# A bias spread and a padding copy moved, and identity products placed in the gaps of a decoder kernel's filling and emptying steps

## The reference

```python
x = x + L0_attn(layernorm(x))                  # self attention, window of +-32 tokens, biases
x = x + L0_xattn(ctx, ctx, layernorm(x), pad)  # cross attention, a padding mask an item, biases
x = x + L0_ffn(layernorm(x))                   # 8 experts, best 2 of a token
x = x + L1_attn(layernorm(x))                  # self attention, causal, no biases
x = x + L1_xattn(layernorm(x), ctx, ctx, mask) # cross attention, one mask, biases
x = x + L1_ffn(layernorm(x))                   # gate, up and down, quantised and dequantised
```

## Time and profile before

| what | value |
|---|---|
| median of 3 runs | 2112.07 us (2107.06 to 2112.2) |
| the profiled execution | 2101.48 us |
| its span, first to last instruction | 2099.7 us |
| its mean granted TensorE clock | 0.975 |
| TensorE busy, share of the span | 93% |
| VectorE, ScalarE, GpSimd busy | 59%, 47%, 33% |

### The profile page before, as it was taken

One profiled execution on the slowest core, in us unless ns is written; L12 is line 12 of the kernel. 1 busy time (PEld: TensorE's weight loads), 2 busy tenths in 40 slices (PEclk: granted clock), 3 DMA queues, 4 the chain that ended last, 5 costly groups with the idle time before them and its releaser, 6 DMA issues. The chain is left out here.

```text
span 2099.7 us, 57083 instructions
## 1 busy us (share of the span) xinstructions
PE 1948.5 (93%) x19802; PEld 1597.3 (76%) x19802; DVE 1233.8 (59%) x5200; ACT 979.4 (47%) x1905; POOL 686.7 (33%) x1244
## 2 busy tenths in 40 slices
PE   7999998999959999999999789999899998999889
PEld 5788886777749999999999578887677775444377
DVE  5788885676541111111115588998778886369964
ACT  2555555676613333333333255556566663357400
POOL 2666665256560000000001545553422220013400
PEclk8999999999969999999999999999999999999999
DMA  7333332334339999999995534433233330000023
GB/s 217 110 109 112 120 129 83 103 113 135 104 120 402 376 339 344 344 340 341 339 343 221 176 119 146 130 125 128 88 96 114 110 108 27 0 0 0 0 71 91
DMA packets 209555, 334.74 MB, mean 159 GB/s; under 512 B 59502, under 2 KB 193427, under 8 KB 200307
## 3 DMA queue, kind: packets, MB, share of 16 engines
q1 hardware_dynamic: 194914, 301.82, 41.6%
q0 software_dynamic: 9552, 26.10, 4.1%
q10 hardware_dynamic: 4928, 4.72, 0.7%
HBM read 193.74 MB, written 28.05 MB: 106 GB/s over the span
## 5 line engine op out<-in xcount | busy, mean ns | idle before, releaser
L2369 ACT ACTIVATE moe_h<-moe_h_ps,moe_weights 128x128 f32<-128x128 f32 x424 | 132.8, 364 | 255.5 <-PE moe_h_ps L2337 226.0
L2802 PE MATMUL ffn_prod_ps<-x_sb,ffn_weights 128*128 128x512 f32 x480 | 209.4, 596 | 7.0 <-ACT ffn_sig_q L2788 7.0
L2401 DVE TENSOR_TENSOR moe_y<-moe_y_ps,moe_weights 128x256 f32<-128x256 f32 x53 | 22.5, 425 | 328.1 <-PE moe_y_ps L2349 328.1
L2280 POOL DMA_DIRECT2D moe_y_dram<-moe_y x71 | 39.4, 555 | 491.4 <-DVE moe_y L2401 483.2
L1403 ACT ACTIVATE causal_prob<-causal_ps 128x768 f32<-128x768 f32 (+1 forms) x192 | 168.8, 879 | 63.0 <-PE causal_ps L1726 62.2
L2337 PE MATMUL moe_h_ps<-moe_h,moe_weights 128*128 128x128 f32 x1696 | 198.0, 275 | 0.0
L2337 PEld LDWEIGHTS moe_h_ps<-moe_h,moe_weights 128*128 128x128 f32 x1696 | 193.6, 192 | 0.1
L2802 PEld LDWEIGHTS ffn_prod_ps<-x_sb,ffn_weights 128*128 128x128 f32 x480 | 90.6, 191 | 123.6 <-issue 109.3
L1072 DVE CUSTOM_DVE_ANT_0 causal_masked<-causal_ps,causal_causal_mask 128x256 bf16<-128x256 f32 (+1 forms) x512 | 151.9, 353 | 28.6 <-PE causal_ps L1692 27.7
L1072 DVE CUSTOM_DVE_ANT_0 window_masked<-window_ps,window_window_mask 128x160 bf16<-128x160 f32 x512 | 135.1, 320 | 46.3 <-PE window_ps L1692 44.9
L1692 PE MATMUL causal_ps<-k_pair,q_pair 64*128 64x78 f32 (+2 forms) x1024 | 102.2, 299 | 20.5 <-DVE causal_m_tok L1072 9.3
(11 more groups left out here) (424 smaller groups left out, 4753.4 us busy)
## 6 DMA issues: line engine op xcount, KB each, us to landing
moe_weights<-moe_w_in SPq DMA_DIRECT2D x53, 2180.0 KB, 9.8
q_pair<-parts SPq DMA_DIRECT2D x512, 128.0 KB
parts<-moe_w_in SPq DMA_DIRECT2D x17, 2180.0 KB, 9.1
k_pair<-parts SPq DMA_DIRECT2D x256, 128.0 KB
k_pair<-parts SPq DMA_DIRECT2D x256, 38.5 KB
moe_y_dram<-moe_y POOLq DMA_DIRECT2D x71, 128.0 KB, 4.0
moe_rows<-moe_slots_dram SPq DMA_DIRECT2D x53, 128.0 KB, 3.7
x_before_ffn_dram<-x_sb SPq DMA_DIRECT2D x16, 256.0 KB, 2.1
```

The source lines that it names most:

```text
L2280: pool.dma_start(route.y_dram[bass.ds(j * TM, TM), :].rearrange("(s p) d -> p s d", p=P), y[r][:])\
L2369: nc.scalar.activation(out[:, f, :], psum[:, f // 2, (f % 2) * TM:(f % 2) * TM + TM], ACT.Gelu, bias=bias[:, f:f + 1]).then_inc(done, 1)
L2802: op = nc.tensor.matmul(prod_ps[:, slot, f, :].rearrange("p (b t) -> p b t", b=2), w[:, k, at:at + P], x_cols(n // GROUPS, k), start=(k == ...
```

## The change

Four edits. (1) `widen` keeps only the spread of bv and runs a slot earlier; the copy of the finished bias is a new function `keep_bias` in the old slot. (2) `padding` stands in slot 3 in all steps. (3) In step 1 of each call, ahead of slots 1 and 2, TensorE makes 5 identity products behind a wait for the values of item 0, and in step 18, ahead of slot 0, 5 more behind a wait for the turned outputs of item 14. (4) The 4 and 2 identity products around `turn_outputs` depend on `ref >= N + 2` alone, and so are made in step 34 of the first call too; the second call has them as before. The words that go with the change speak of fewer products in emptying steps; the code takes none away.

```diff
-        START_WARM, END_WARM, LOAD_WARM, DRAIN_WARM = 16, 13, 6, 4
+        START_WARM, END_WARM, LOAD_WARM, DRAIN_WARM, FILL_WARM = 16, 13, 6, 4, 5
...
-                        if i == 3 and wide(ref):
+                        if i == 3:
                             padding(t, ref)
...
-                    if not wide(ref):
-                        padding(t, ref)
...
                         nc.vector.tensor_copy(bv_wide, L.bv[:].unsqueeze(2).to_broadcast([P, KC, P])).then_inc(widened, 1)
-                        dve.wait_ge(bias_mm, n + 1)
+
+                def keep_bias(r):
+
+                    L = layers_in[r]
+                    if L.biased:
+                        dve.wait_ge(bias_mm, with_bias.index(L) + 1)
                         nc.vector.tensor_copy(L.out_bias[:], bias_ps(r)).then_inc(bias_done, 1)
...
+                        if ref < NL and i == bias_slot(ref) - 1:
+                            widen(ref)
                         if ref < NL and i == bias_slot(ref):
-                            widen(ref)
+                            keep_bias(ref)
...
-                    if emptied(ref):
+                    if ref >= N + 2:
                         keep_warm(DRAIN_WARM, ps2)
...
-                    if i == 7 and emptied(ref) and active(ref, 3):
+                    if i == 7 and ref >= N + 2 and active(ref, 3):
                         keep_warm(DRAIN_WARM // 2, ps2)
...
+                        if ref == 1 and i in (1, 2):
+                            pe.wait_ge(v_ev, t)
+                            keep_warm(FILL_WARM, psb)
+                        if i == 0 and ref == B + 2:
+                            pe.wait_ge(oT_ev, t - 3)
+                            keep_warm(FILL_WARM, psb)
```

## The result

| | before | after |
|---|---|---|
| median of 6 runs | 2110.98 us (2106.28 to 2114.17) | 2092.09 us (2088.89 to 2099.12) |
| ratio, 95% interval | | 0.9931 [0.9911, 0.9950] |
| the profiled execution | 2101.48 us, mean clock 0.975 | 2095.83 us, mean clock 0.980 |

The change is faster, by 14.6 us (10.5 to 18.8) by the ratio of the runs; the two medians are 18.9 apart. Forecast were 9.4 us off 2112.07, that is 2102.7 in a range of 2097 to 2111.

A forecast was written before the change was run, and what follows sets the result against it. TensorE was taken as the bound, at half clock behind gaps in steps 1 and 18. Terms 3.5 + 2.3 + 2.2 + 1.1 + 0.3 = 9.4 us off the 2112.07 median gave 2102.7 us, range 2097 to 2111.

The forecast's parts named there:

- What bounds the kernel: TensorE, busy 93% of the span, at half clock behind waits in step 1 and step 18 of both calls.
- The spread: Step 1: spreading bv a slot earlier removes 0.99 us of idle time before the first call's bias product.
- Step 1, first call: Identity products ahead of slots 1 and 2 hold the clock: 3.5 us gained, bounds 0.5 and 3.95.
- rival 2: The clock holds through step 1 but falls in step 2; one new fall leaves 7.1 us, two 4.8; chance 0.16.
- the prediction's own sign of being wrong: Among the signs listed as showing the forecast wrong: new stretches at half clock in steps 2 and 3 of either call.
- Step 1, second call: Identity products in the waits ahead of slots 1 and 2 hold the clock: 2.3 us gained, bounds 0 and 2.4.
- Step 18: Identity products in the waits at its start hold the clock: 2.2 us gained in the first call, 1.1 in the second.
- Rival 1: The clock falls in step 18 all the same and only step 1 gains: 6.1 us, 2106.0 us; chance 0.15.
- What was said for the forecast there: At step 17's start TensorE waited 2.08 us behind the same turning of outputs, and the clock had not fallen.
- Padded rows: Step 17's start: copying the row in slot 3 shortens the 2.08 us wait until the stacked q is late; 0.3 us.
- Step 34: First call: added products at half clock make TensorE 1.0 us late, but this is covered: 0, bounds -1.0 and 0.
- the last one of the sum: The 9.4 us from the profiled execution was assumed the same against the timed median 2112.07, 10.6 above it: 2102.7 us.

The follow-up runs named there:

- e2_more: Two kernels: the whole change plus five identity products at step 17's start, ratio 0.997; that plus two ahead of scores of slots 1 to 3 in step 2, 0.9956.

## Why the prediction missed

**What bounds the kernel: right.** TensorE at half clock at the named places, and it is their products with the spread that bring the gain (-10.3 without the other two edits).

**The spread: right.** 0.99 was worked out for the first call, 1.0 is what two profiles without it lose in step 1.

**Step 1, first call: right at its place, too high for its neighbourhood.** 3.5 worked out; from ScalarE's copy for item 1 to that for item 2 it is 3.9 us less than in the profiled execution in all nine profiles that have five products and the spread. But three of the six profiles without products show 3.4 us of half clock there for 6.8, and are 2.2 to 2.5 shorter themselves; against the mean of the six the gain is 2.7. And rival 2 came on top, as the prediction's own sign of being wrong: in 11 of the 12 profiles with products in step 1 steps 2 and 3 show a fall, 6.8 us in ten of them for 3.4 in the profiled execution. From the copy for item 2 to that for item 4, the eight profiles with five products and the spread, and none in step 2, are 1.5 longer than the profiled execution on average (1.0 to 2.1) and 0.9 longer than the mean of the six. What is left of 3.5 is 2.4 or, against the mean, 1.8. Rival 2 had 2.3 for such a fall.

**Step 1, second call: mis-sized.** 2.3 worked out against the profiled execution. In the six other profiles without products there, this step took 1.5 us longer on average than in that execution (-0.9 to +3.6); in seven with products and spread (all but the two e2_more kernels) it took 2.5 less (0.5 to 3.8). The term is nearer 4 than 2.3: the step's cost was read from one execution in which its fall was short (6.8 us at half clock, where four of the other six show 10.2 or more).

**Step 18: right at its place.** First call 2.2 worked out: from the turned rows to the products with v, seven profiles without products take 6.4 to 6.8 us, eight with them 4.3, and three in which 3.4 us of half clock are left 6.0. Second call 1.1 worked out; from ScalarE's copy for item 18 to that for item 19, seven profiles without products against eight with: 1.2 apart. In the time of a kernel without the products of step 1 none of it arrives (+0.8 and -0.4). Rival 1, the fall at step 18 all the same, is refuted for the first call in eight of eleven profiles and for the second call in all ten. What was said for the forecast there, that the clock had stood at the start of step 17 behind 2.08 us of waiting, was the weakest reason: in 12 of 16 profiles without products at that place the clock does fall there or just before. The Trainium skill ("TensorE: Matmul & The Clock Gate", Part 4: PE-mode transpose) has transposes not keep the clock up; by the 4 profiles in which it stood behind the same transposes and the 12 in which it didn't, these runs neither bear the rule out nor refute it.

**Padded rows: right in kind.** The wait passed to the stacked q and is as long as before (2.11 for 2.08): 0.0 for 0.3. **Step 34: right**, 0, with the products at half clock and nobody waiting.

**The step that failed is the last one of the sum, and the range made from it.** "I assume that the sum is the same there" set the 9.4 us worked out in one profiled execution against a median of three timed runs 10.6 above it, and the low end against the lowest of these three. So the 10.6 were carried over to the changed kernel, and there they were not: its timed median lies 3.7 below its profiled execution. In the series of the result the kernel before stayed at 2110.98, and it is the gain that came out larger, 14.6 (10.5 to 18.8) for 9.4. In the later series it is the level that was lower. The kernel before ran 110 times more in four series: medians 2103.77 to 2105.57, runs from 2097.62 to 2114.69. Of the 110, 105 lie below 2112.07, and 79 below the shortest of the first three. Set against the median of a series, the same sum gives 2094.4 to 2096.2; the whole change measured 2095.02 and 2092.82. The profiled execution alone would have done as well: 2101.48 less 9.4 is 2092.1, as the prediction says in the line before it leaves that number.

That the sum fits so well is luck in part. Its term for step 1 of the first call was too high by 1 to 2 us and that for the second call too low by about as much, and measured alone its parts bring far less than they were given. The range took in the costs of the places and rivals, and of the scatter of one and the same kernel only the 5 us of three runs: it is 16 us from the shortest to the longest of 29 runs, more than the change is worth. (The chance of a faster kernel adds up to 0.60 by its own parts, not 0.58; nothing hangs on it.) The Trainium skill ("TensorE: Matmul & The Clock Gate", Part 1: The HAM clock gate) says that the number of slow matmuls at a start varies from run to run and advises not to fit to one count. The first fall of these profiles, at 9 to 17 us, varies likewise: 6.8, 3.4 or 0 us in code that no kernel here changes.

**What stays open.** Why the first series gave 14.6 us where two later ones gave 10.5 and 10.9. The intervals overlap (0.9911 to 0.9950 and 0.9933 to 0.9963), so scatter may be enough. But all six timed runs of the kernel before stood at 2106.28 or above there, as only 38 of the 110 later ones did, and that isn't explained: no profile was taken of such a run. And why the parts gain less alone than together.

## What to carry to other kernels

Where a clock rises and falls within the execution, read each place's cost from several profiles, and set the sum of the places against the median of many runs, not of three; a profile is one draw. A few filler products in a gap can hold the clock at that place, in most executions, but look at the next step for the fall that moves there. A part that brings nothing alone can still be needed: try the whole before taking parts out.

## What the runs showed of the hardware

- The same code runs at half clock at other places from one execution to the next: steps 16 and 17 of the first call had 0 us of it in one profile of the kernel before and 13.7 us in another.
- Five identity products (ten in one kernel) held the clock at most of the places where they stand: no half clock in step 1 of the first call in 12 of 12 profiles, and in step 18 of the second call in 10 of 10. In step 18 of the first call it was 8 of 11, in step 1 of the second call 6 of 11; in the others 3.4 us were left.
- Half clock costs by its place. From ScalarE's copy for item 31 to the identity products behind the routing scores, the 14 profiles without a fall in the last wide steps have 26.9 to 36.9 us of half clock and take 82.4 to 82.7 us; the three with 6.8 us of it in those wide steps take 85.4 to 85.5. Over the runs of the kernel before, a mean clock higher by 0.001 goes with 1.0 to 1.6 us less, by series.
